# An attention and mixture-of-experts layer on one core: the orders of the first and last blocks and of the passage to the experts, and the experts' down projection by feature

## The reference

```python
q, k, v = silu(x @ Wq), silu(x @ Wk), x @ Wv        # 16 heads of 8 features
q, k = rotated(q), rotated(k)                       # [t*cos, t*sin]: 16 features a head
energy = (q @ k.T) * lower_triangle                 # linear attention, no softmax
out = layernorm((energy @ v) @ Wo * sigmoid(x @ G1 @ G2)) * gamma + beta
x = layernorm(x + out)
# feed-forward: 8 experts, two for each token, 1280 places in each expert
w = renormalised two best of softmax(rmsnorm(x) @ router_w.T)
routed[token] += w * ((silu(xg @ rg[e]) * (xg @ ru[e])) @ rd[e])     # inner width 512
shared = (silu(x @ sg) * (x @ su)) @ sd                              # inner width 1024
x = layernorm(x + shared + routed)
```

## Time and profile before

| | |
|---|---|
| three runs | 858.65, 870.18, 861.96 us; median 861.96 |
| the profiled execution | its own time 858.42 us, span 856.6 us |
| granted TensorE clock, mean | 0.987 |
| PE busy in the span | 808.4 us, 94% |

### The profile page before, as it was taken

The page is one execution under the profiler, slowest core; times in us unless marked ns, Lnnn a source line. Parts: engine busy times, 40 slices in busy tenths (PEclk is TensorE's granted clock), DMA queues, the critical chain, the costliest instruction groups (busy, mean ns, idle before and its releaser), DMA issues.

```text
span 856.6 us, 27882 instructions
## 1 busy us (share of the span) xinstructions
PE 808.4 (94%) x11178; PEld 658.8 (77%) x11178; DVE 611.7 (71%) x1941; ACT 355.7 (42%) x744; POOL 400.2 (47%) x375
## 2 busy tenths in 40 slices
PE   5989999999999999999999898889999999999995
PEld 3667787777777777777777676668999999998875
DVE  6576978979797897979788988864445444443675
ACT  6333544535445453535443332223333333222575
POOL 7522141333224133323415545464487787777433
PEclk9899999999999999999999999999999999999998
DMA  5135111111121111112122221032345555433454
GB/s 146 30 108 209 39 51 44 43 45 42 37 52 49 42 44 45 43 39 52 39 60 54 66 48 46 3 107 81 79 96 96 97 100 97 65 51 31 124 159 136
DMA packets 74095, 59.89 MB, mean 70 GB/s; under 512 B 10163, under 2 KB 63722, under 8 KB 73968
## 3 DMA queue, kind: packets, MB, share of 16 engines
q1 hardware_dynamic: 56944, 41.84, 17.5%
q0 software_dynamic: 17024, 16.28, 10.5%
HBM read 23.99 MB, written 28.89 MB: 62 GB/s over the span
## 4 chain that ended last, share of the span: by engine, by line
PE 78%; DVE 12%; issue 4%; POOL 2%; DMA 1%; ACT 1%; DVEq 0%; POOLq 0%; ACTq 0%; SPq 0%
PE bank L1671 6%; PE bank L1673 5%; PE bank L1672 5%; PE energy_banks L1730 5%; PE energy_and_gate_banks L1671 5%; PE bank L1775 4%; PE bank L2190 4%; PE energy_and_gate_banks L1755 4%; PE energy_and_gate_banks L2190 4%; PE energy_and_gate_banks L1673 3%; PE energy_and_gate_banks L1672 3%; PE energy_banks L1671 3%; PE energy_banks L1673 3%; PE energy_banks L1672 3%; PE energy_banks L1723 2%
## 5 line engine op out<-in xcount | busy, mean ns | idle before, releaser
L559 POOL DMA_INDIRECT dispatched_rows<-x,slot x128 | 131.2, 1025 | 199.8 <-PE energy_banks L1730 113.6
L671 POOL DMA_INDIRECT summed_rows<-VP,goal_i x80 | 124.4, 1555 | 42.0 <-issue 22.5
L1001 ACT ACTIVATE sq<-energy_banks 128x512 f32<-128x512 f32 (+1 forms) x96 | 50.6, 527 | 120.0 <-PE energy_banks L1673 118.3
L1143 DVE TENSOR_TENSOR sf<-sf,bank 128x512 f32<-128x512 f32 x88 | 60.4, 686 | 38.0 <-PE bank L1673 36.7
L629 POOL TENSOR_TENSOR rr<-vq,minus_half 128x8 f32<-128x8 f32 x16 | 26.7, 1668 | 103.5 <-DVE vq L1213 103.5
L743 ACT ACTIVATE hidden_rounded<-sf 128x512 fp32r<-128x512 f32 x88 | 55.5, 631 | 39.2 <-DVE sf L1143 39.2
L733 ACT ACTIVATE sf<-energy_and_gate_banks 128x512 f32<-128x512 f32 x88 | 52.7, 599 | 35.3 <-PE energy_and_gate_banks L1673 32.4
L1115 DVE TENSOR_TENSOR EM<-energy_and_gate_banks,causal 128x512 f32<-128x512 f32 x64 | 44.0, 688 | 26.8 <-PE energy_banks L1755 20.8
L706 ACT ACTIVATE sq<-bank 128x512 f32<-128x512 f32 x64 | 38.3, 599 | 48.4 <-PE bank L1673 46.0
L1775 PEld LDWEIGHTS bank<-VP,Kt 64*64 64x64 f32 x896 | 35.5, 134 | 29.3 <-issue 17.9
L1730 PE MATMUL energy_banks<-EM,VP 64*32 64x64 f32 x4096 | 56.6, 229 | 0.0
(11 more groups left out here) (239 smaller groups left out, 2264.2 us busy)
## 6 DMA issues: line engine op xcount, KB each, us to landing
QM<-QT SPq DMA_DIRECT2D x248, 32.0 KB
dispatched_rows<-empty POOLq DMA_DIRECT2D x8, 655.0 KB
QM<-dispatched_rows SPq DMA_DIRECT2D x8, 655.0 KB, 5.8
xin<-in_x SPq DMA_DIRECT2D x16, 256.0 KB, 2.8
QM<-summed_rows SPq DMA_DIRECT2D x16, 256.0 KB, 2.8
out_x<-QM SPq DMA_DIRECT2D x16, 256.0 KB, 3.2
summed_rows<-empty SPq DMA_DIRECT2D x13, 256.0 KB, 2.0
dispatched_rows<-x,slot POOLq DMA_INDIRECT x128
```

The source lines that it names most:

```text
L559: g.indirect_dma_start(out=xg_d, out_offset=bass.IndirectOffsetOnAxis(ap=slot[:, n % 2, j:j + 1], axis=0), in_=x1[:, n % 2, j % NC, :], in ...
L671: g.indirect_dma_start(out=sum_d, out_offset=bass.IndirectOffsetOnAxis(ap=goal_i[:, par, t:t + 1], axis=0), in_=ye[:, par, t, :], in_offse ...
L1143: v.tensor_tensor(sf[:, n % SF], sf[:, n % SF], UB[:], ALU.mult).then_inc(v_h, 1)
```

## The change

1. **Opening.** The products for the cosine table are made on DVE (`table_product`, `table_sum`), no longer on POOL. ACT makes the fourth silu ahead of the values. Block 1's input is turned, rounded and given its remainder at the end of the opening, in a bank of its own (`input_bank`).
2. **Block 1.** `centre` moves ahead of the third mask on DVE.
3. **Blocks 12 to 15.** `shared_hidden` moves up in the row of work of DVE; `slots` of blocks 12 to 14 moves to the start of the next step; `positions` no longer waits for the last state there, and in block 15 it stands two pieces of work earlier on PE; block 15's `mean_square` moves to the passage, its routing earlier.
4. **Dispatch.** A dispatch waits for the empty table (`g_fill`), not for the landing of all earlier dispatches; the landings are counted by parity. The first transfer of block 13's rows goes ahead of a small power.
5. **Passage.** Orders of PE, ACT and DVE are changed (below); `sd_s` now lies over `th` and its load also waits for `v_y`.
6. **Experts.** `down` is by feature: the weights are stationary, the hidden values (now hi and lo) move, and the result, with features on partitions, is copied to SBUF by ACT and turned back by PE (`back`). `wd` is split once an expert by ACT and DVE. DVE's product goes to `sf` in place; `rows(0)` moves behind the group 2's last product, `rows(2)` into the next expert's first group.

```diff
@@ SP, step 16 @@
                     keep_sum(SPARE, DIRECT)
+                    sp.wait_ge(v_y, B)
                     sp.dma_start(sd_s, sd.rearrange("(f p) d -> p f d", p=P)).then_inc(sd_ld, 16)
@@ POOL, dispatch @@
-                    need(gp, g_sc, P * (n - 1))
+                    need(gp, g_fill, P)
@@ DVE, opening @@
-                    for i in (0, 1):
-                        link(v.tensor_tensor(by_place[:, i], coarse[0][:, i], fine[1][:, i], ALU.mult))
+                    table_product(0)
                     table_sum(0)
+                    table_product(1)
                     turn(f, fp, 0)
...
                     turn(f, fp, 3)
+                    input_lo(1)
@@ DVE, first_blocks @@
                     if back:
                         gate_moments(b)
+                        centre(b)
                     mask(b, par, 2)
                     mask_state(b, 5)
                     turn(f, fp, 2)
                     turn(f, fp, 3)
                     if back:
-                        centre(b)
                         add_input(b)
@@ PE, last_block @@
                     down_by_column(SPARE, (4,))
+                    positions(b)
                     states_and_out(3)
                     down_by_column(SPARE, (5,))
                     energies_and_state(3)
                     down_by_column(SPARE, (6, 7))
-                    positions(b)
@@ PE, positions @@
-                need(pe, v_S, NS * (last(b) + 1))
                 if no_ffn(b):
                     need(pe, v_h, 8 * SPARE + spare_turn(b, 1) + 1)
                     need(pe, v_lg, b - 1)
+                else:
+                    need(pe, v_S, NS * (last(b) + 1))
@@ ACT, experts @@
+                def copy_down(n):
+                    w = P * GROUPS[n][1]
+                    need(act, e_dn, 3 * e + n + 1)
+                    need(act, e_bk, 3 * e + n - 1)
+                    a.activation(oT[:, (n + par) % 2, 0:w], (OB, SBK)[(n + par) % 2][:, 0:w], ACT.Copy).then_inc(e_cp, 1)
@@ DVE, experts @@
+                def hidden_lo(n, f):
+                    k = 12 * e + 4 * n + f
+                    hp, w = (n + par) % 2, P * GROUPS[n][1]
+                    need(dve, e_hh, k + 1)
+                    v.tensor_tensor(he_lo[:, hp, f, 0:w], sf[:, k % SF, 0:w], he_hi[:, hp, f, 0:w].bitcast(f32),
+                                    ALU.subtract).then_inc(e_hl, 1)
...
+                        if n == 2 and f == 3:
+                            rows(0)
@@ PE, experts @@
+            def back(n, e):
+
+                hp = (n + e) % 2
+                need(pe, e_cp, 3 * e + n + 1)
+                for c in range(GROUPS[n][1]):
+                    ins = t.transpose((OB, SBK)[hp][:, P * c:P * (c + 1)], oT[:, hp, P * c:P * (c + 1)], ident[:])
+                ins.then_inc(e_bk, 1)
...
+                        if f == 1 and n == 0 and e > 0:
+                            back(2, e - 1)
...
-                    for c in range(GROUPS[n][1]):
-                        for f in range(4):
-                            ins = t.matmul((OB, SBK)[hp][:, P * c:P * (c + 1)], he[:, hp, f, P * c:P * (c + 1)],
-                                           wd[:, par, f], start=(f == 0), stop=(f == 3))
+                    for f in range(4):
+                        need(pe, e_hl, 12 * e + 4 * n + f + 1)
+                        hi, lo = he_hi[:, hp, f, 0:w], he_lo[:, hp, f, 0:w]
+                        t.matmul(bank, wd_hi[:, par, f], hi, start=(f == 0), stop=False)
+                        t.matmul(bank, wd_hi[:, par, f], lo, start=False, stop=False)
+                        ins = t.matmul(bank, wd_lo[:, par, f], hi, start=False, stop=(f == 3))
                     ins.then_inc(e_dn, 1)
...
                 down(0)
                 gate_up(2)
+                back(0, e)
                 if e == E - 1:
                     turn_late(1)
                 down(1)
                 down(2)
+                back(1, e)
```

More of the change, by code:

```diff
@@ L625, in step @@
                     first_rstd(b)
+                if b == B - 1:
+                    dispatch(b, (0,))
                 if within(b, 1, B):
@@ L644, in step @@
                 if b >= B - 1:
-                    dispatch(b, range(2 * NC))
+                    dispatch(b, range(b == B - 1, 2 * NC))
             stage1(gp, step, range(-1, B + 2))
@@ L789, in opening @@
                     a.activation(wvg_hi, wvg_s, ACT.Copy).then_inc(a_wvg, 1)
-                    for i in (0, 1, 2):
+                    for i in range(4):
                         silu(f, fp, i)
@@ L1534, in _ @@
             slots(B + 1, 1)
-            rows_lo(AGAIN)
-            shared_add(RELOADED, x1t[:, 1])
             for f in range(8):
@@ L2224, in group @@
                     ff = slice(P * f, P * (f + 1))
+                    if g == 0 and f == 1:
+                        back(2, E - 1)
                     need(pe, a_sf, n - 1)
```

248 lines of the change are left out of this document (155 added, 93 removed).

## The result

The changed kernel takes 866.18 us in the median of 20 runs (863.34 to 871.49), before takes 861.24 (855.92 to 870.67) in as many. The ratio is 1.007, 95% interval 1.0052 to 1.0088: 6 us slower, where 1 to 5 us faster was forecast. It lies on the wrong side of before and outside the forecast's own range of 850 to 863, though inside the wider one of 846 to 868.

What follows compares the result with a forecast made beforehand. PE, busy 94% of the span, was taken to bound the kernel with its waits. From 858.4 us, -3.5 - 2 - 6 + 8.7 + 1 = -1.8 gives 856.6, said as 857; own range 850 to 863 (0.66), 8 in 10 846 to 868.

Steps and rivals of the forecast that it cites:

- opening and block 1: Opening: two PE waits and part of a half-clock stretch go, -3.5 us (-1.5 to -5.5); block 1: -2 (-0.7 to -2.8).
- the blocks' term: Blocks 12 to 15: PE's 4.5 us of waits at the positions and half clock behind them go, -6 us (-3 to -8).
- The passage's mechanism: Passage: later spare addition delays store and `sd_s` load, PE idles up to ten us, experts start 8.7 us later.
- the upper bound of 11: Passage: +11 us instead of +8.7 if PE's ten us of idle time bring the clock to half behind them.
- about 16: Passage, a sign of being right: the last dispatch comes about 16 us after the start of the spare addition.
- The first rival: Passage: the load of `sd_s` does not bind, -1 us in place of +8.7, total 847; chance 0.16.
- The experts and the tail: Experts' periods -2 us, tail +3 us, together +1 us (-3 to +5).
- have room: Experts: DVE, busy 11 of 24 us, and ACT, busy 8, can take the added remainders and copies.
- The tail's +3 for the scatters: Tail: later `rows(0)` makes the last expert's scatters end later, so PE waits longer for reloaded sums, +3 us.
- The second rival: Experts: DVE and POOL hold each other up, cycle 25.7 us against 23.97, 13 us more, 869 to 870; chance 0.12.
- Block 1's -2: Block 1: moving `centre` ahead of the mask removes PE's 1.8 us wait and some half clock, -2 us (-0.7 to -2.8).
- The upper bound: Whole kernel: the terms' bounds added without luck give 867 us or so, with luck 846.

Runs made afterwards that it cites:

- after_again: The changed kernel, unchanged, run again in a group where before took 874 to 876 us: 1.0072 of before (1.0041 to 1.0104).
- passage_alone: The kernel before with only the passage's new orders of PE, ACT and DVE: 1.0143 of before (1.0091 to 1.0195), 12.5 us slower, six runs.
- opening_alone: The kernel before with only the opening's change: 0.9975 of before (0.9945 to 1.0005), 2 us faster.
- opening_block1_again: The kernel before with only the changes to the opening and block 1, run a second time: 0.9953 of before (0.9925 to 0.998).
- sd_first: The changed kernel with the load of `sd_s` issued on SP ahead of the store of the spare sum: 1.0004 of before (0.9964 to 1.0045).
- opening_block1: The kernel before with only the changes to the opening and block 1: 0.9959 of before (0.9932 to 0.9986), 3.5 us faster.
- spare_alone: The kernel before with only the change to blocks 12 to 15, block 15's mean square first in the passage: 0.9969 of before (0.9944 to 0.9993).

## Why the prediction was wrong

| term | forecast | shown by runs |
|---|---|---|
| opening and block 1 | -5.5 | -3.5 and -4.0 (two groups) |
| blocks 12 to 15 | -6 | -2.7 alone, -0.5 on top of the others |
| passage | +8.7 | +12.5 alone, of it 8.3 (6 in the whole) the load of `sd_s` |
| experts and tail | +1 | +3.5 alone |
| the whole | -1.8 | +6 |

The terms taken alone don't add up to the whole: they make 9 to 12. From the last attention output to expert 0's rows it takes 59.1 us in after_again, with part 3, and 59.2 in passage_alone, without it. So what part 3 gives back in the passage does not come on top of part 5, by estimate 2 to 3 us of the excess (50.4 to 52.1 us there in the four traces with parts 1 to 3 or 1 to 4, 48.4 in opening_alone). The rest lies within the interval of passage_alone and is not settled.

**The failing step is the blocks' term**, "I take -6 (-3 to -8)" out of "at most 4.5 + 3.4 = 7.9". I took PE's wait at the positions and the half clock behind it as the prize and let DVE's idle time cap it, though that idle time was at another place of the block. The wait did go. But DVE, with as much work as before, was late at the next things it was asked for: the state (1.65, 0.96) in the blocks, x1 in the passage (3.2 for 2.0). Measured were -2.7 alone and -0.5 on top of the opening, both outside the bounds of -3 to -8. The new order of slots and mean square at the head of the passage was counted nowhere, though PE's first wait there hangs on it.

**The passage's mechanism was right and is the best-shown step**: the addition behind the hiddens, then store, load, PE's ten us of idle time (9.8), landing at about 569. Relative to the last attention output the addition came 6.5 later, I said 7.2, and expert 0's rows 10.9 later against 8.7; the upper bound of 11 named one reason, half the clock behind the idle time (5.1 for 3.6 in the down projection). The last dispatch came 21.6 behind the addition; the prediction's own sum has 18.8 there (584.2 less 565.4), and the "about 16" among its signs doesn't fit that sum. It stood 7.7 above its old time and not 3 below it, since the blocks ahead brought 3.1 and not 11.5. What the order costs beside the load, some 4 us, was not in the term as such. The first rival, that the load does not bind, is refuted from both sides.

**The experts and the tail** were mis-sized by 2.5. The replaced part gave the 0.8 that was forecast (7.17 for the down projections and not 6.97, but 0.85 for the turnings back and not 1.1 to 1.3). The period gave 0.3. The step that failed is "have room": DVE had 18.6 us of work in a period, and PE waits 0.24 for its product in each expert. The tail's +3 for the scatters was right (10.2 against 7.1), but I had no term for the sum's wait behind it.

**The second rival, contention of DVE and POOL, is weak here**: POOL's splits grew by 0.7 us an expert, where 2.8 were reckoned with; the period is PE's, and the forecast of 25.7 us is off by two. Its mechanism is there, but smaller: few of DVE's remainders run beside a split, and those that do take 0.97 for 0.69, or with 256 columns up to 0.65 for 0.42. The rule of the Trainium skill ("SBUF — State Buffer", "Who interferes with whom") would have the one that comes second held until the first is done. This trace agrees in part: the remainder of `wd`, which starts 0.18 behind the cast, is lengthened by 0.28, but it ends before the cast does, and the cast, which came first, is lengthened too, by 0.42.

**The opening** came at 43.3 as forecast, and its stretch of half clock (22 to 29 us) is gone, but the baseline was a single execution, late by 1 to 3 us against five of seven other kernels with the same opening. Block 1's -2 is within what its traces scatter, 28.4 to 33.1 us for the same code, and its half clock stayed, at 66.7 to 70.1 us.

**The upper bound** was added up wrong: the poor ends of the five terms (-1.5, -0.7, -3, +11, +5) make 10.8 on 858.4, that is 869 and not "867 or so". The measured 866.18 lies inside.

The best kernels of the study leave out parts 4 to 6: parts 1 and 2 alone stood at 0.9959 and 0.9953 of before, 4 us faster, and parts 1 to 3 at 0.9947 beside the latter, but at 0.999 in another group.

## What to carry to other kernels

When an operation is moved back on one engine, look for the in-order queue that stands on it and for everything behind it there: here one addition held a store, the store a weight load, and the load PE for 9.8 us; issuing the load first gave back nearly the whole loss of the changed kernel. When a wait of the busiest engine is taken away, ask first whether the engine that it waited for has less work afterwards; if it only has another order, expect the wait under another name. And take what a wait costs from several traces: terms of 2 to 4 us are within what the same code differs from one execution to the next.

## What was not expected of the hardware

The same kernel before took 859 or 860 us in two groups and 874 to 876 in three, and the profiles of the latter groups differ in blocks 12 to 15 above all: with before's code there, from block 11's gate to the last attention output it takes 101.2 us in opening_alone, against 93.6 in the profile of before and 93.9 in opening_block1_again. PE's lists in these groups hold 8 to 11 stops there that nothing releases, up to 1.19 us and 2.4 to 4.4 us in all (in passage_alone 3, of 1.2 in all); those of the two groups at 859 and 860 one or none. Two more things go with it. The granted clock over this stretch was 0.90 in after_again and sd_first and 0.93 in opening_alone, and 0.96 to 0.98 in before, the changed kernel and opening_block1_again; but opening_block1, of a group at 859, also had 0.90 there and took 99.1 us with one stop. And each trace of the three groups has 18 to 38 signals of PE that are recorded more than 0.6 us behind the modelled end of their matmul, up to 5.0 us; those of the other groups, of before and of the changed kernel have one or none. In sd_first, for one line of PE:

```profile
PE energy_banks L1812 <- issue: 2.7, 8, 0.4
```

One group at 859 and one at 874 are recorded under the same chip number (14), so the chip alone doesn't make this. What does is not shown.

The granted clock fell to half (1.2 of 2.4 GHz) behind waits of 1.04, 2.04, 2.11, 2.9, 3.8 and 9.8 us in the changed kernel's trace, for about 3 us of PE's work each time. It did not fall behind the wait of 1.65 at 473.39 (1.00 from 471 to 477 us), while in spare_alone it did behind one of 1.66. It fell also to 0.53 from 453 to 456 us, where no wait over 0.32 stands ahead of it. A part of it comes and goes whatever the order of the instructions is, and must be left out when a wait is priced.
